# Adding the last experts' block results into two DRAM tables by indirect transfers, in place of storing them and gathering them

## The chip, the cores and the metric

The kernel runs on one core of one Trainium2 chip. The metric is the device time of one launch in microseconds (us). The kernel before takes 2686.56 us, the median of 3 runs (2667.9, 2686.56 and 2697.57).

## The reference, cut to what matters

Two layers run over 4096 tokens of width 256 (32 tiles of 128). Each layer is an attention followed by a mixture of experts. The change is in the last stage, the second mixture: 16 experts with hidden width 256, 4 chosen for each token, and in the attention before it, which routes the first 20 tiles.

```python
# z = x + attention; h = rms(z) * ff_ln_w
# scores = h @ wg;  top 4 of 16;  weights = softmax over the 4 chosen
# per token: y = sum over the 4 experts e of weight_e * (silu(h @ w1[e]) * (h @ w3[e])) @ w2[e]
# out = skip + tanh(g_ffn) * (z + y)
```

So every token gets four rows of expert output, each times its weight, added to its own row z.

## The kernel before, in words

The five stages run one after the other: softmax attention, first experts (8 experts, 2 chosen), linear attention, causal attention, last experts. Routing sorts tokens by expert: a token's normalised row is written by GpSimd (POOL) with an indirect transfer (`Router.send`, L360) to four places in the DRAM table `moe_rows`, one for each chosen expert, so that each expert's tokens stand in whole blocks of 128 rows. Places that no token takes keep the zeros that the softmax stage wrote there. The last experts have two parts: 20 tiles routed in the causal stage (95 blocks) and 12 tiles routed while the first part is computed (63 blocks); 158 blocks in all. The 12 tiles' rows need 48 sends.

One loop over blocks b is written out by hand on each engine of `experts`; there is no scheduler. TensorE (PE) in iteration i turns the rows of block i+2 (`turn_rows`, L1403, into `moe_pt`), does the gate and up products of i+1 (`up`, L1416, `moe_pgu`), turns the activation of i (`turn_act`, L1424) and does the down product of i-1 (`down`, L1435, `moe_py`). ScalarE (ACT) and VectorE (DVE) split the turned rows into a high and a low part (L1248, L1333), form silu times up (L1253, L1338), and DVE copies the block's result from PSUM into `moe_ys` (L1344, three buffers). SyncE (SP) loads block rows into `moe_xs` (`load_rows`, L1081, three buffers, behind a wait for `turn_rows` three blocks earlier).

ACT stores each block's result to a DRAM table (L1265). When all blocks of a part are stored, POOL gathers, for each tile and each k of 4, the 128 result rows by the tokens' slot numbers (`gather`, L1174, into `moe_yg`), and DVE combines (`combine`): four multiply-adds with the weights `wk` (L1315) and one with the gate and the skip row (L1323). SP loads z and skip (L1085, L1087) and stores the output (L1091). The first part's 20 tiles are combined between the blocks of the second part, one every second block, the second part's 12 tiles after the last block. For the first three of these 12 tiles (`HELD` is 3) POOL gathers rank by rank as soon as the experts concerned are stored (`limits`, `until`, L1202 to L1204). The weights `wk` by rank come from `share` and four times `share_of` (L338 to L343), in `weigh`.

## Time and profile before

| | |
|---|---|
| median of 3 runs | 2686.56 us |
| the profiled execution | 2682.36 us |
| its span | 2680.6 us |
| busy: PE, DVE, ACT, POOL | 2266.7, 1855.2, 1159.6, 1103.8 us |
| last experts, from its first instructions | from 2137 us to the end, 544 us |

The profiled execution's own time is 1.76 us over its span, and 4.2 us under the median. Times in the views are counted from the span's start. A row of a timeline gives the start, the duration, the engine, the line of the kernel, what is written and read, and in brackets how long the engine was idle before and what ended that. "DMA to landing" is counted from the start of the issuing instruction to the transfer's completion.

### The profile page before, as it was taken

The numbers are of one execution on the slowest core, as the hardware profiler recorded it, in microseconds if no ns is written. First come the engines' busy times: TensorE is split into PE (matmuls) and PEld (weight loads), VectorE is DVE, ScalarE is ACT, GpSimd is POOL, SyncE is SP. The second block draws the span as 40 slices with busy tenths as digits, with TensorE's granted clock in tenths as the row PEclk, the third lists the DMA queues.
The fourth block names the chain that finished last, engine by engine and source line by source line (L and its number), as shares of the span: only waits on it lengthen the run. The fifth ranks groups of instructions, "written<-read, shape, count | busy, mean of one in ns | idle before, by whom it ended". The sixth has DMA issues, their size and how long they took to land. (4 is left out here: it accounts for less than half of the span.)

```text
span 2680.6 us, 60407 instructions
## 1 busy us (share of the span) xinstructions
PE 2266.7 (85%) x20880; PEld 1718.4 (64%) x20880; DVE 1855.2 (69%) x3965; ACT 1159.6 (43%) x2509; POOL 1103.8 (41%) x1111
## 2 busy tenths in 40 slices
PE   6899999885887689995799998999988698999990
PEld 4555555543766567773577877777767577887770
DVE  4888888872556757765778788788787365445754
ACT  2676667664533223333344444444333263333330
POOL 3454445464153500000454454455477600224626
PEclk9897779865888889997999999999989799999995
DMA  5455555442368431201322323322334472446754
GB/s 118 120 115 129 143 129 135 114 125 87 113 215 252 150 134 41 60 29 40 88 66 75 84 66 78 81 72 73 76 96 116 136 240 79 138 137 184 234 159 144
DMA packets 249859, 313.10 MB, mean 117 GB/s; under 512 B 45152, under 2 KB 202848, under 8 KB 249056
## 3 DMA queue, kind: packets, MB, share of 16 engines
q1 hardware_dynamic: 188592, 219.11, 29.3%
q0 software_dynamic: 26624, 58.79, 8.0%
q10 hardware_dynamic: 34352, 31.34, 3.5%
q8 instruction: 180, 2.95, 0.5%
q14 instruction: 111, 0.91, 0.1%
HBM read 122.40 MB, written 102.24 MB: 84 GB/s over the span
## 5 line engine op out<-in xcount | busy, mean ns | idle before, releaser
L2084 POOL TENSOR_TENSOR ca_qk<-ca_qk,ca_q_swap 128x512 f32<-128x512 f32 x160 | 249.3, 1558 | 366.5 <-DVE ca_q_swap L2262 366.2
L731 DVE TENSOR_REDUCE soft_top<-soft_pa 128x2 fp32r<-128x512 f32 x512 | 328.1, 683 | 101.2 <-PE soft_pa L811 98.1
L626 ACT ACTIVATE soft_prob<-soft_pb 128x512 f32<-128x512 f32 x512 | 285.7, 594 | 190.4 <-PE soft_pb L804 187.9
L804 PE MATMUL soft_pb<-soft_rep 25*128 25x256 f32 x1024 | 210.2, 378 | 46.5 <-DVE soft_top L731 27.0
L804 PEld LDWEIGHTS soft_pb<-soft_rep 25*128 25x128 f32 x1024 | 137.3, 225 | 169.6 <-issue 85.3
L1416 PE MATMUL moe_pgu<-moe_w_hi,moe_xt_hi 128*128 x472 | 196.1, 415 | 38.9 <-DVE moe_xt_lo L1333 30.1
L811 PE MATMUL soft_pa<-soft_rep 24*128 24x256 f32 x1024 | 219.2, 384 | 5.8 <-DVE soft_top L731 3.5
L1435 PE MATMUL moe_py<-moe_w_d,moe_at 128*128 x788 | 217.8, 392 | 1.5 <-issue 0.8
L1338 DVE TENSOR_TENSOR moe_act_f<-moe_silu,moe_pgu 128x256 f32<-128x256 f32 (+1 forms) x236 | 88.4, 375 | 151.0 <-ACT moe_silu L1253 150.4
L2353 PE MATMUL ca_py<-ca_w_hi,ca_ot_hi 128*128 128x256 f32 x512 | 157.6, 308 | 35.0 <-DVE ca_ot_lo L2283 34.8
L1253 ACT ACTIVATE moe_silu<-moe_pgu 128x256 f32<-128x256 f32 (+1 forms) x236 | 82.1, 348 | 230.6 <-PE moe_pgu L1416 230.3
L825 PE MATMUL soft_po<-soft_prob,soft_vaug 128*32 128x256 f32 x2048 | 175.7, 473 | 0.0
L2262 DVE TENSOR_TENSOR ca_q_swap<-ca_q_swap,ca_sin_q 128x512 f32<-128x512 f32 x128 | 118.3, 924 | 80.8 <-DMA ca_q_swap<-ca_q_f 80.6
L1416 PE MATMUL moe_pgu<-moe_w_hi,moe_xt_lo 128*128 x472 | 174.1, 369 | 0.0
L1416 PE MATMUL moe_pgu<-moe_w_lo,moe_xt_hi 128*128 x472 | 173.7, 368 | 0.0
L2146 ACT ACTIVATE ca_ot_hi<-ca_po 128x512 fp32r<-128x512 f32 x128 | 69.5, 595 | 209.3 <-PE ca_po L2451 209.3
L1174 POOL DMA_INDIRECT moe_yg<-moe_ys_rows,moe_held x112 | 113.2, 1011 | 111.1 <-DVE moe_ys L1344 32.3
L360 POOL DMA_INDIRECT moe_rows<-moe_x_new,moe_held x80 | 78.1, 976 | 195.1 <-DVE moe_ys L1344 118.1
L2353 PE MATMUL ca_pp<-ca_ht_hi,ca_w_hi 128*128 128x512 f32 x312 | 138.7, 444 | 23.1 <-ACT ca_q_f L2132 19.6
L1333 DVE TENSOR_TENSOR moe_xt_lo<-moe_pt,moe_xt_hi 128x256 fp32r<-128x256 f32 x236 | 99.4, 421 | 74.8 <-ACT moe_xt_hi L1248 73.4
L2353 PE MATMUL ca_py<-ca_w_lo,ca_ot_hi 128*128 128x256 f32 x512 | 150.9, 295 | 0.0
L2353 PE MATMUL ca_py<-ca_w_hi,ca_ot_lo 128*128 128x256 f32 x512 | 150.6, 294 | 0.0
(377 smaller groups left out, 6376.3 us busy)
## 6 DMA issues: line engine op xcount, KB each, us to landing
ca_q_swap<-ca_q_f SPq DMA_DIRECT2D x640, 64.0 KB
moe_xs<-moe_rows SPq DMA_DIRECT2D x236, 128.0 KB, 2.1
soft_rep<-soft_parts SPq DMA_DIRECT2D x378, 64.0 KB
moe_rows<-soft_blank SPq DMA_DIRECT2D x27, 768.0 KB, 3.7
...
```

The lines of the kernel that those rows point to most:

```text
L626: act.activation(prob[:, k % 4, h, :], p_b[:, 2 * T * h:2 * T * (h + 1)], ACT.Exp).then_inc(prob_ready, 1)
L731: dve.tensor_reduce(heads[:, j, :, g], p_a[:, 2 * T * h:2 * T * (h + 1)].rearrange("p (c s) -> p c s", c=HALF), AX, ALU.max).then_inc(a_do ...
L804: mm = pe.matmul(p_b[:, out], rep[of, i % 4, g, at:at + PART], rep[of, i % 4, g, 0:T], start=True, stop=True)
L811: mm = pe.matmul(p_a[:, out], rep[of, n % 4, g, at:at + PART], rep[of, n % 4, g, T:2 * T], start=True, stop=True)
L825: mm = pe.matmul(p_o[g % 2][32 * j:32 * j + 32, 0:T], vaug[:, i % 4, sc, 4 * g + j, :], prob[:, (2 * g + j // 2) % 4, j % 2, sc * T:(sc + ...
L1174: pool.indirect_dma_start(out=yg[:, t % HELD, k, :], out_offset=None, in_=ys_rows[h], in_offset=bass.IndirectOffsetOnAxis(ap=slot_id[:, t, ...
L1333: dve.tensor_tensor(xt_lo[:, b % 2, :, :], p_t[b % 2][:, 0:DIM].rearrange("p (k t) -> p k t", k=KC), xt_hi[:, b % 2, :, :].bitcast(fp32), ...
L1416: mm = pe.matmul(p_gu[b % 2][:, 0:W2], x[:, b % 2, k, :], w, start=(n == 0), stop=(n == 3 * KC - 1))
L1435: mm = pe.matmul(p_y[b % 2][:, 0:DIM], at[:, b % 2, m, :], w_d[:, bass.ds(e, 1), m, :].rearrange("p a d -> p (a d)"), start=(m == 0), stop ...
L2084: pool.tensor_tensor(qk[:, u % 2, m, :], qk[:, u % 2, m, :], q_swap[:, p % 2, :], ALU.add).then_inc(qk_ready, 1)
L2262: dve.tensor_tensor(out.rearrange("p (b s) -> p b s", s=SEQ), src.rearrange("p (b s) -> p b s", s=SEQ), tab[int(m == RQ)][:].unsqueeze(1). ...
L2353: mm = pe.matmul(out, x, y, start=start and n == 0, stop=stop and n == len(todo) - 1)
```

## The change

- The weight goes with the row. A sent row of the last experts is now 273 words wide (`WIDE`): 256 values, its token's 16 weights by expert, and its token's number as an integer. `place` is followed at once by `share`, which writes weights and numbers into the rows; `share_of` and `limits` are gone for these experts.
- DVE evacuates a block with a multiplication by the weight column of the block's expert (L1405), taken with a register that it loads for each block (L1401), where it copied before.
- POOL adds the block's 128 result rows to a DRAM table by the token numbers in the block's rows (L1239, an indirect transfer with add). Even blocks add into table 0, odd ones into table 1. An add is issued behind a wait that the add two blocks earlier, into the same table, has landed (`out_of`). Table 0 holds z, written by the causal stage; table 1 is zeroed. Rows that no token took have weight zero and a number of 0 to 127, rows of padding ahead of the tokens.
- `moe_xs` has six buffers, since the number and the weights are read from it until the add is done; SP loads block b's rows behind a wait that block b-6 has been added, no longer behind `turn_rows`. DVE writes `moe_ys` of block n when block n-3 has been added.
- A tile's combination is one addition of the two tables' rows (L1367) and the operation with gate and skip (L1369); SP loads three tiles for it in place of two. ACT stores nothing, POOL gathers nothing.
- The softmax stage clears 23 pieces in place of 32. The causal stage fills the wide table with blank rows, three blocks at a time, in its first 53 steps, from SP. `until`, `reached` and the early gathers are gone.

In the fences below a row is one instruction in an engine's order of issue; `x` with a number means as many alike in a row. POOL, from the third `rstd` of the last experts' routing on, before and after:

```order
L167 TENSOR_TENSOR moe_r_rstd<-moe_r_var,moe_r_half_neg 128x4 x3
L360 DMA moe_rows<-moe_x_new,moe_held 8448x256 x48
L1174 DMA moe_yg<-moe_ys_rows,moe_held 128x256 x80
L1202 TENSOR_LOAD moe_until
L1202 ISA x2
L1204 TENSOR_TENSOR moe_spare<-moe_r_half_neg 1x1
L1174 DMA moe_yg<-moe_ys,moe_held 128x256 x3
```

```order
L368 DMA moe_rows<-moe_x_new,moe_held 8064x273
L1239 DMA moe_sums<-moe_ys,moe_xs 3072x256
L368 DMA moe_rows<-moe_x_new,moe_held 8064x273
L1239 DMA moe_sums<-moe_ys,moe_xs 3072x256 x17
L1239 DMA moe_sums<-moe_ys,moe_xs 2304x256 x63
```

The 48 sends stood in a row, paced by block results; they now alternate with the adds of blocks 30 to 78. 128 gathers became 158 adds.

DVE, the last blocks and what follows them (before, then after):

```order
L1333 TENSOR_TENSOR moe_xt_lo<-moe_pt,moe_xt_hi 128x256
L1338 TENSOR_TENSOR moe_act_f<-moe_silu,moe_pgu 128x256
L1344 COPY moe_ys<-moe_py 128x256
L1315 SCALAR_TENSOR_TENSOR moe_xd<-moe_yg,moe_held,moe_xd 128x256 x4
L1323 SCALAR_TENSOR_TENSOR moe_xd<-moe_xd,moe_gate,moe_sk 128x256
```

```order
L1389 TENSOR_TENSOR moe_xt_lo<-moe_pt,moe_xt_hi 128x256
L1394 TENSOR_TENSOR moe_act_f<-moe_silu,moe_pgu 128x256
L1401 TENSOR_LOAD moe_held
L1401 ISA x2
L1405 ISA
L1405 TENSOR_SCALAR moe_ys<-moe_py,moe_xs 128x256
```

A load of the expert's number into a register now stands between the activation and the evacuation of each block.

SP after its last load of rows (before, then after):

```order
L1091 DMA out<-moe_xd 128x256
L1085 DMA moe_xd<-scratch 128x256
L1087 DMA moe_sk<-scratch 128x256
L1091 DMA out<-moe_xd 128x256
```

```order
L1112 DMA moe_sk<-scratch 128x256 x5
L1120 DMA moe_xd<-moe_sums 128x256
L1120 DMA moe_xb<-moe_sums 128x256
L1132 DMA out<-moe_xd 128x256
L1112 DMA moe_sk<-scratch 128x256
L1120 DMA moe_xd<-moe_sums 128x256
L1120 DMA moe_xb<-moe_sums 128x256
L1132 DMA out<-moe_xd 128x256
```

The pair of table loads stands five times ahead of the first store; then store and three loads alternate seven times, and five stores end it.

The diff, cut to its core:

```diff
@@ -326,8 +325,14 @@
         dve.wait_ge(route, ticks.n)
         dve.reciprocal(wsum[:], wsum[:]).then_inc(route, ticks.one())
         dve.wait_ge(route, ticks.n)
-        dve.tensor_tensor(weight[:], weight[:], wsum[:].unsqueeze(2).to_broadcast([PART, n, E]), ALU.mult
-                          ).then_inc(route, ticks.one())
+        if self.carry:
+            dve.tensor_tensor(self.rows[:, :, DIM:DIM + E], weight[:], wsum[:].unsqueeze(2).to_broadcast([PART, n, E]), ALU.mult
+                              ).then_inc(self.wk_ready, 1)
+            dve.tensor_scalar(self.rows[:, :, DIM + E:].rearrange("p t o -> p (t o)").bitcast(U32), self.thr[:, 1:n + 1],
+                              self.order[:], None, ALU.add).then_inc(self.ids_ready, 1)
+        else:
+            dve.tensor_tensor(weight[:], weight[:], wsum[:].unsqueeze(2).to_broadcast([PART, n, E]), ALU.mult
+                              ).then_inc(route, ticks.one())
 
     def share_of(self, dve, k):
...
 
-        to = self.c["moe_rows"][self.h]
+        to = self.c[self.stage + "_rows"][self.h]
         if first == 0:
             pool.wait_ge(self.idx_ready, 1)
+            if self.carry:
+                pool.wait_ge(self.wk_ready, 1)
+                pool.wait_ge(self.ids_ready, 1)
         for n in range(first, min(last, self.n * self.TOP)):
             t, k = divmod(n, self.TOP)
...
@@ -1048,10 +1065,17 @@
             linear = LinearAttention(ahead, st)
         LATE = FIRST[1]
 
+        OUT = len(ys_out)
+
         def written(eng, blocks):
 
-            for i in range(3):
-                eng.wait_ge(ys_out[i], 16 * ((blocks - i + 2) // 3))
+            for i in range(OUT):
+                eng.wait_ge(ys_out[i], 16 * ((blocks - i + OUT - 1) // OUT))
+
+        def out_of(eng, b):
+
+            if b >= 0:
+                eng.wait_ge(ys_out[b % OUT], 16 * (b // OUT + 1))
 
         def combined_behind(b):
 
...
@@ -1077,14 +1101,31 @@
                     n = b - START[h]
                     if b == START[1]:
                         sp.wait_ge(route.sent, 16 * NEW * TOP)
-                    past(sp, xt_mm, b - 2)
-                    sp.dma_start(xs[:, b % 3, :], xs_rows[h][n * PART:(n + 1) * PART]).then_inc(xs_in[b % 3], 16)
+                    if adds:
+                        out_of(sp, b - XS)
+                    else:
+                        past(sp, xt_mm, b - 2)
+                    sp.dma_start(xs[:, b % XS, :], xs_rows[h][n * PART:(n + 1) * PART]).then_inc(xs_in[b % XS], 16)
+
+                def load_skip(t):
+                    past(sp, stored[t % SUMS], 16 * (t // SUMS))
+                    sp.dma_start(sk[:, t % SUMS, :], skip[t]).then_inc(xd_in[t % SUMS], 16)
+
+                def load_tables(t):
+                    h = int(t >= FIRST[1])
+                    if t == FIRST[h]:
+                        written(sp, START[h] + BLOCKS[h])
+                    at = PART * (t - FIRST[h] + 1)
+                    for dst, src in ((xd, tables[h][0]), (xb, tables[h][1])):
+                        sp.dma_start(dst[:, t % SUMS, :], src[at:at + PART, :]).then_inc(xd_in[t % SUMS], 16)
 
                 def load_sum(t):
+                    if adds:
+                        load_skip(t)
+                        load_tables(t)
+                        return
                     past(sp, stored[t % SUMS], 16 * (t // SUMS))
                     sp.dma_start(xd[:, t % SUMS, :], x_in[t]).then_inc(xd_in[t % SUMS], 16)
-                    if norm == "rms":
-                        sp.dma_start(sk[:, t % SUMS, :], skip[t]).then_inc(xd_in[t % SUMS], 16)
 
                 def store_sum(t):
                     sp.wait_ge(final, t + 1)
...
@@ -1144,8 +1187,14 @@
                 for t in behind:
                     if t not in [combined_behind(b - STORE_LAG) for b in range(ALL)]:
                         store_sum(t)
-                    if t not in [combined_behind(b - LOAD_LAG) for b in range(ALL)] and t + SUMS < TILES:
+                    if not adds and t not in [combined_behind(b - LOAD_LAG) for b in range(ALL)] and t + SUMS < TILES:
                         load_sum(t + SUMS)
+                if adds:
+                    for t in range(LATE, LATE + SUMS):
+                        load_skip(t)
+                    for t in range(LATE, LATE + SUMS):
+                        load_tables(t)
+
                 def last_sum(n):
                     t = LATE + n
...
                     ).then_inc(yg_in[t % HELD], 16)
 
+                if adds:
+                    for b in range(ALL):
+                        g = behind(b, MEASURE)
+                        if g is not None:
+                            route.root(pool, g)
+                        if b > PLACE:
+                            route.send(pool, b - PLACE - 1, b - PLACE)
+                        pool.wait_ge(y_ready, b + 1)
+                        out_of(pool, b - 2)
+                        h = part_of(b)
+                        pool.indirect_dma_start(
+                            out=tables[h][b % 2], out_offset=bass.IndirectOffsetOnAxis(
+                                ap=xs[:, b % XS, DIM + EXPERTS:].bitcast(U32), axis=0),
+                            in_=ys[:, b % 3, :], in_offset=None, bounds_check=tables[h][b % 2].shape[0] - 1, oob_is_err=True,
+                            compute_op=ALU.add).then_inc(ys_out[b % 2], 16)
+                    return
                 route.send(pool, 0, NEW * TOP, (y_ready, PLACE, START[1] - PLACE - 4))
                 pool.wait_ge(route.sent, 16 * NEW * TOP)
...
@@ -1298,8 +1349,11 @@
                             route.tally(dve)
                     if b == PLACE:
                         route.place(dve)
-                        route.limits(dve, until[:], START[1] + 3, until_ready)
-                    if b == WEIGH:
+                        if adds:
+                            route.share(dve)
+                    if b == WEIGH and adds:
+                        route.name_experts(dve)
+                    if b == WEIGH and not adds:
                         route.weigh(dve)
                         if norm == "layer":
                             dve.wait_ge(route.wk_ready, TOP)
...
                             dve.wait_ge(gated, 1)
 
                 def combine(t):
-                    dve.wait_ge(xd_in[t % SUMS], (32 if norm == "rms" else 16) * (t // SUMS + 1))
+                    dve.wait_ge(xd_in[t % SUMS], (48 if adds else 16) * (t // SUMS + 1))
+                    row = xd[:, t % SUMS, :]
+                    if adds:
+                        dve.tensor_tensor(row, row, xb[:, t % SUMS, :], ALU.add).then_inc(added, sums.one())
+                        dve.wait_ge(added, sums.n)
+                        dve.scalar_tensor_tensor(out=row, in0=row, scalar=gate[:], in1=sk[:, t % SUMS, :],
+                                                 op0=ALU.mult, op1=ALU.add).then_inc(final, 1)
+                        return
                     dve.wait_ge(yg_in[t % HELD], 16 * TOP * (t // HELD + 1))
-                    row = xd[:, t % SUMS, :]
                     for k in range(TOP):
                         past(dve, added, sums.n if k else 0)
                         op = dve.scalar_tensor_tensor(out=row, in0=yg[:, t % HELD, k, :], scalar=wk[:, t, k:k + 1], in1=row,
                                                       op0=ALU.mult, op1=ALU.add)
-                        if norm == "layer" and k == TOP - 1:
+                        if k == TOP - 1:
                             op.then_inc(final, 1)
                         else:
                             op.then_inc(added, sums.one())
-                    if norm == "rms":
-                        dve.wait_ge(added, sums.n)
-                        dve.scalar_tensor_tensor(out=row, in0=row, scalar=gate[:], in1=sk[:, t % SUMS, :],
-                                                 op0=ALU.mult, op1=ALU.add).then_inc(final, 1)
...
@@ -1339,9 +1395,17 @@
                                           p_gu[(b + 1) % 2][:, HIDDEN:W2], ALU.mult).then_inc(act_ready, 1)
                     if b >= 1:
                         n = b - 1
+                        if adds:
+                            if n == START[1]:
+                                dve.wait_ge(route.expert_ready, 1)
+                            e = dve.value_load(expert_of[0:1, n:n + 1], min_val=0, max_val=EXPERTS - 1)
                         dve.wait_ge(y_mm, n + 1)
-                        past(dve, ys_out[n % 3], 16 * (n // 3))
-                        dve.tensor_copy(ys[:, n % 3, :], p_y[n % 2][:, 0:DIM]).then_inc(y_ready, 1)
+                        out_of(dve, n - 3)
+                        if adds:
+                            dve.tensor_scalar(ys[:, n % 3, :], p_y[n % 2][:, 0:DIM], xs[:, n % XS, DIM:DIM + EXPERTS][:, bass.ds(e, 1)],
+                                              None, ALU.mult).then_inc(y_ready, 1)
+                        else:
+                            dve.tensor_copy(ys[:, n % 3, :], p_y[n % 2][:, 0:DIM]).then_inc(y_ready, 1)
                     routing(b)
                     t = combined_behind(b)
                     if t is not None:
...
@@ -2048,13 +2121,21 @@
                     if summed(n) is not None:
                         old, h = summed(n)
                         sp.wait_ge(zn_ready, 2 * old + h + 1)
-                        sp.dma_start(z_out[old * TPC + 2 * h:old * TPC + 2 * h + 2].rearrange("t p d -> p t d"),
+                        at = old * TPC + 2 * h
+                        part = int(at >= SENT)
+                        at = PART * (at - part * SENT + 1)
+                        sp.dma_start(c["moe1_sums"][part][0][at:at + 2 * PART, :].rearrange("(t p) d -> p t d", p=PART),
                                      z[:, old % ZB, 2 * h:2 * h + 2, :]).then_inc(stored[h], 16)
                     new = fresh(n, 0)
                     if new is not None and new >= 1:
                         load_x(new)
                     if n == 0:
                         held.load(sp)
+                        sp.wait_ge(blank_in, 16)
+                    if 0 <= n < len(empty):
+                        h, to = empty[n]
+                        sp.dma_start(to.rearrange("(r p) d -> p r d", p=PART),
+                                     blank[:].unsqueeze(1).to_broadcast([PART, to.shape[0] // PART, WIDE])).then_inc(emptied[h], 16)
                     if n == STEPS - 1:
                         sp.wait_ge(qk_ready, M5 * UNITS)
```

## Rows read from the trace of the kernel before

**Rows 1.** The page: the chain that ended last, share of the span by line.

```profile
PE moe_pgu L1416 7%; PE moe_py L1435 4%; DVE moe_xd L1315 2%; PE moe_pat L1424 1%; PE moe_pt L1403 1%; POOL moe_yg L1174 1%; DVE moe_xt_lo L1333 0%; DMA moe_xs<-moe_rows 0%; PE moe_py L211 0%; DMA moe_yg<-moe_ys,moe_held 0%; DVE moe_ys L1344 0%; PE moe_py L193 0%; PE moe_py L252 0%; DMA moe_ys<-moe_ys 0%; DVE moe_xd L1323 0%
```

**Rows 2.** Windows of L1344, one copy for each block: stretch, length, copies' busy time, clock, DMA share, GB/s.

```profile
2151.30:2187.53 36.23, 5.51 (x13) 1.00 0.94 314
2187.53:2283.02 95.49, 10.11 (x24) 0.95 0.28 90
2283.02:2452.28 169.26, 26.75 (x63) 1.00 0.44 142
2452.28:2575.71 123.43, 16.83 (x40) 1.00 0.76 226
2575.71:2613.32 37.61, 5.94 (x14) 1.00 0.41 126
```

**Rows 3.** Timeline of one block's period in the first part.

```profile
2298.94 0.38 PE L1403 MATMUL moe_pt<-moe_held,moe_xs 128*128 128x128 f32 x2
...
2300.77 1.03 PE L1435 MATMUL moe_py<-moe_w_d,moe_at 128*128 x4
...
2301.17 0.42 DVE L1338 TENSOR_TENSOR moe_act_f<-moe_silu,moe_pgu 128x256 f32<-128x256 f32 x1 [0.96 <-ACT moe_silu L1253]
2301.64 0.38 PE L1403 MATMUL moe_pt<-moe_held,moe_xs 128*128 128x128 f32 x2
...
2301.84 0.42 DVE L1344 COPY moe_ys<-moe_py 128x256 f32<-128x256 f32 x1 [0.25 <-PE moe_py L1435]
...
2303.03 0.97 POOL L360 DMA_INDIRECT moe_rows<-moe_x_new,moe_held  x1 [4.40 <-DVE moe_ys L1344]
```

**Rows 4.** Lines L1081 and L360 in 2300 to 2400: issues (duration in ns), then landing.

```profile
L1081 SPq DMA_DIRECT2D moe_xs<-moe_rows x37: 319/320/320, 2302.0 to 2398.8; - x37
DMA to landing us min/median/max: 2.0/2.1/3.6
...
L360 POOL DMA_INDIRECT moe_rows<-moe_x_new,moe_held x29: 971/972/974, 2303.0 to 2397.1; - x29
DMA to landing us min/median/max: 2.6/2.7/4.4
```

**Rows 5.** Line L1174, the gathers, in 2580 to 2610: issues, then landing.

```profile
L1174 POOL DMA_INDIRECT moe_yg<-moe_ys,moe_held x9: 998/1007/1010, 2587.9 to 2606.7; - x9
DMA to landing us min/median/max: 2.8/3.1/4.5
```

**Rows 6.** Line L1081 in 2150 to 2250, then in 2460 to 2570.

```profile
DMA to landing us min/median/max: 2.0/3.5/7.5
...
L1081 SPq DMA_DIRECT2D moe_xs<-moe_rows x36: 319/319/430, 2461.3 to 2569.8; - x36
DMA to landing us min/median/max: 2.1/2.9/4.0
```

**Rows 7.** Timeline of DVE: the first and the last operation of `share_of` in the last experts.

```profile
2267.81 0.36 DVE L338 TENSOR_TENSOR moe_r_left<-moe_r_key,moe_r_top 128x192 f32<-128x192 f32 x1
...
2272.32 0.35 DVE L343 TENSOR_REDUCE moe_held<-moe_r_left 128x12 f32<-128x192 f32 x1
```

**Rows 8.** Timeline of the end: last block's copy, one store and the loads behind it, the last gather.

```profile
2617.85 0.42 DVE L1344 COPY moe_ys<-moe_py 128x256 f32<-128x256 f32 x1 [0.44 <-PE moe_py L1435]
...
2661.37 0.34 SPq L1091 DMA_DIRECT2D out<-moe_xd  x1
...
2663.12 0.32 SPq L1085 DMA_DIRECT2D moe_xd<-scratch  x1
2663.49 0.43 SPq L1087 DMA_DIRECT2D moe_sk<-scratch  x1
...
2671.76 1.13 POOL L1174 DMA_INDIRECT moe_yg<-moe_ys,moe_held  x1 [0.30 <-issue]
2674.86 2.05 DVE L1315 SCALAR_TENSOR_TENSOR moe_xd<-moe_yg,moe_held,moe_xd 128x256 f32<-128x256 f32 x4 [2.84 <-DMA moe_yg<-moe_ys,moe_held]
2676.94 0.48 DVE L1323 SCALAR_TENSOR_TENSOR moe_xd<-moe_xd,moe_gate,moe_sk 128x256 f32<-128x256 f32 x1
```

**Rows 9.** Causal stage: line L338, and DVE's waits for the swapped halves; softmax stage: its clears.

```profile
L338 DVE TENSOR_TENSOR ca_r_left<-ca_r_key,ca_r_top x4: 476/482/486, 1968.1 to 2014.2; 128x320 f32<-128x320 f32 x4
...
DVE ca_q_swap L2262 <- DMA ca_q_swap<-ca_q_f: 80.6, 64, 3.6
...
moe_rows<-soft_blank SPq DMA_DIRECT2D x27, 768.0 KB, 3.7
```

162 lines of the change are left out of this document (82 added, 80 removed).

## The prediction

> **What bounds the kernel now.** I read the page's chain of waits first. In the last experts it runs through TensorE, with DVE's combinations and POOL's gathers behind [rows 1]. Then the windows over the copies of L1344, of which each block has one; they give the block's period by stretch [rows 2]: 36.23 / 13 = 2.79 us while the weights are prepared (A), 95.49 / 24 = 3.98 with the routing of the last 12 tiles (B), 169.26 / 63 = 2.69 in the rest of the first part (C), 123.43 / 40 = 3.09 where 20 combinations lie between the blocks (D), 37.61 / 14 = 2.69 after these (E). 2.69 is TensorE's own work: the turning of a block starts at 2298.94 and the next one's at 2301.64 [rows 3]. D's blocks are 0.40 longer, as a combination is five DVE operations. The other limit is the end [rows 8]: the last copy ends at 2618.27, the span at 2680.6, so 62.3 us follow in which TensorE is idle and POOL's gathers set the pace.
>
> **The end.** The change removes 39 late gathers and four of the five multiply-adds. In its place: the last add. It is issued 0.77 us after its copy (2302.26 to 2303.03 in [rows 3]) and takes 2.7 + e to land, where 2.7 is a plain indirect write of the same 128 rows [rows 4] and e what the add costs more. The last three copies come close together, so the last add also waits for the one two before: about 7.0 us in all at the e = 1.05 that I take below. Then SP issues ten table loads, 4.1 us at 0.32 to 0.43 each, before its first store. For seven tiles it then does a store, waits 1.75 us from the store's start until it has landed (2661.37 to 2663.12 [rows 8]) and issues three loads, 0.37 + 0.43 + 0.43: 2.98 a tile, 20.9 in all. A load lands in 2.1 [rows 4], the two DVE operations take 0.9, and from the last operation's end (2677.42) to the span's end there are 3.2 [rows 8]. Sum 7.0 + 4.1 + 20.9 + 2.1 + 0.9 + 3.2 = 38 against 62: **-24**. Here SP takes POOL's place as the bound.
>
> **The ring of six buffers.** This is the change's price, and nothing in the diff's wording says it. SP may load block b's rows only when block b-6 is added. Before, the load waited for the turning of b-3, and the copy, ACT's store and the gathers were beside the path. Now copy, add and load form a loop with TensorE's order. Its parts: from the start of a turning to the end of that block's copy, three periods, 3 x 2.69 = 8.07, and from the start of the fourth iteration to the copy's end 3.32 (2298.94 to 2302.26 [rows 3]); copy to issue on POOL 0.77; landing 2.7 + e; the load of the rows 2.1 [rows 4], after which the turning of b starts. With 0.2 for the register load (below) that is 17.16 + e. The loop spans six blocks, and six blocks of TensorE's work are 16.1. So even at e = 0 it is 1.0 too long, and the period becomes (17.16 + e) / 6. With the shortest landings seen in these rows (2.6, 2.0) and no register load it is 2.80.
>
> **What the add costs.** No row shows one. The least is e = 0, a plain indirect write, 2.7. The most is a gather followed by a write with one issue: a gather lands in 3.1 [rows 5], less its issue of 1.0, so e = 2.1. The add must read its destination before it writes, but the source is read in the same time, and rows of 1 KB are short against the fixed part. Neither end is nearer; I take the middle, 1.05, and the period is 18.2 / 6 = 3.04. A landing of 2.7 less 1.0 of issue leaves 1.7 in which data moves and is confirmed.
>
> The Trainium skill ("Collectives: The Full Stack", the bandwidth ceiling, on why ReduceScatter is half of AllGather) says that an add in a DMA costs not by its arithmetic but by its second source read, which goes through the same ring and halves the rate. No run here shows it. By it the 1.7 would at most double, e would be at most 1.7, and the sum 15 us higher than mine.
>
> By stretch: C, 63 x (3.04 - 2.69) = **+22**. E, 14 x 0.35 = **+5**. D: landings under load are longer, the rows' load 2.9 in place of 2.1 [rows 6]; the gathers that made most of the load are gone but each tile has a third load and the adds read twice, so I take half, 0.4, for the load and the same for the add: (18.2 + 0.8) / 6 = 3.17 against 3.09, x 40 = **+3**. The gain of the shorter combination (0.40 a block, 16 us) is thus lost to the loop. A: DMA is 94% busy [rows 2] and the rows' load takes 3.5 [rows 6]; with 1.4 more for it and 1.5 for the add the period is 21.1 / 6 = 3.5 against 2.79, x 13 = **+9**. B: long DVE steps let the loop catch up; only the eight intervals of some 2.7 pay 0.35: **+3**.
>
> **The smaller parts.** Weights by rank: the twelve operations of `share_of` take 2267.81 to 2272.67 [rows 7], all of it in TensorE's way, since DVE does its block work behind them; with `limits` gone and the numbers added that is **-5**. `share` only moves from one step to another. The sends on POOL: a send and an add are 0.97 + 0.30 each, 2.5 of a period of 3.04, so they fit, the add starting 0.8 behind its copy as before. The register load on DVE: between the start of the activation and the copy there are 0.67 us (2301.17 to 2301.84 [rows 3]) with DVE idle for 0.25; TensorE has the same load in each block and no gap in [rows 3]. Between nothing and the 1.0 of a POOL issue I take 0.2 of delay. In A, where DVE's four operations already fill the block, it would be seen whole, but the loop's 3.5 covers it. The Trainium skill ("DMA: Bandwidth & Descriptors", latency and other measured facts) gives a register load a floor of about 0.6 us; no row here has one; by it the delay would be 0.35 and the sum 3 us higher. ACT's stores go: nothing, since ACT waited in every block.
>
> The causal stage loses 4 x 3 DVE operations of 0.48, 5.8 us, and gets 53 writes of 419 KB on SP among the half-swaps that DVE waits 80.6 us for [rows 9]. -6 to +10, taken as 0. The softmax stage has 9 clears of 768 KB less of 32, 3.7 us each and hidden [rows 9]: 0, at the least -5. Rows of 1092 in place of 1024 bytes: 7% more on loads of 2.1, hidden in the rounding.
>
> **Sum.** 22 + 5 + 3 + 9 + 3 - 5 - 24 = +13. On the profiled execution's 2682.4 that is 2695. This execution is 4 us under the median of the runs, 2686.6, whose three runs lie 30 us apart, so I leave it at **2695**, no difference that can be told. About 1%, 27 us, is what a measurement of this kernel can tell: faster is under 2660, slower over 2713.
>
> **Rivals.**
> *The forecast*, the six-buffer loop at e from 0 to 2.1: each us of e is 138 periods / 6 = 23 us and 1.5 in the end, so 2670 to 2721, with its centre inside 1%. Chance 0.52.
> *The loop does not bind* (faster): the add lands like a plain write and the loads overlap better than my walk round the loop has it. TensorE keeps 2.69. Then D falls to 2.69 (-16), C, E and B cost nothing, A perhaps +3, end -26 (e = 0), weights -5: -44, 2638. For it: TensorE is 100% in C, and the loop misses by only 1.0 in 16. Against it: the shortest landings in [rows 4] still give 2.80 (and with that 2660). Chance 0.22.
> *The two tables' chain binds* (slower): an add waits until the add two blocks back has landed, so the period is at least (0.77 + 2.7 + e) / 2 = 1.74 + e / 2. It overtakes the loop where 1.74 + e / 2 = 2.86 + e / 6, at e = 3.4, a landing of 6.1; the period is then 3.43: C +47, E +10, D +14, A +9, B +6, weights -5, end -20: +61, 2743, and more beyond. For it: gathers land in up to 4.5 even here [rows 5], and the read before the write comes in no row. Against it: e would be over both bounds. Chance 0.18.
> *The causal stage decides*: the blank writes delay half-swaps by a good part of their worth, or its DVE saving counts: 10 to 20 us to either side of 2695. Chance 0.08.
>
> Faster takes the second rival and a little of the forecast's lower end and of the fourth: 0.24. Slower takes the chain, the forecast's part over e = 1.8 and some of the fourth: 0.31. The rest, 0.45, is within 1%. The range is 2650 to 2740: it holds the forecast's own 2670 to 2721 and leaves out half of the fast case and half of the slow one.
>
> **What would show it.** The evacuations of L1405 in C: 3.04 apart if I am right, 2.69 for the second case, 3.4 for the third. Who releases the turning: the load of the rows in the forecast; in the third case POOL's adds would be issued on the landing of an add, not on the copy. The landing of L1239: 3.7 by my middle. D's period: 3.17. The end: 38 us from the last evacuation, stores 2.98 apart. Wrong would be: a period that stays at 2.69 with adds that land in 3.5 or more, for then my loop has a part that is not there; or a difference in the stages before 2137 us.

## The result, and the profile after

The changed kernel takes **2850.68 us** (median of 4 runs, 2824.22 to 2855.78), the kernel before, on the same chip, 2685.8 (4 runs): 1.060 times as long, 95% interval 1.0512 to 1.0688. I had forecast 2695 with a range of 2650 to 2740, so the forecast is wrong, on the slow side and by 156 us. The profiled execution of the changed kernel took 2855.78 us, its span is 2854.0, against 2680.6 before.

Where the 173.4 us between the two spans lie: the last experts start 5.0 us later (ScalarE's gate at 2142.24, before at 2137.23); from that start to the end of the last evacuation they take 668.9 us, before 481.0 (+187.9); and what follows the last evacuation takes 42.8 us instead of 62.3 (-19.5). So nearly all of it is the pace of the blocks, and the end did gain, though less than forecast.

The page's chain of waits by line, which answers to [rows 1]. First the shares by engine, then by line.

```profile
DMA 11%; PE 7%; issue 3%; DVE 2%; SPq 1%; ACT 0%; DVEq 0%; POOL 0%; POOLq 0%; ACTq 0%
DMA moe_sums<-moe_ys,moe_xs 7%; PE moe_pgu L1477 4%; DMA moe_xs<-moe_rows 4%; PE moe_py L1496 2%; DVE moe_ys L1405 1%; PE moe_pt L1464 1%; DMA out<-moe_xd 1%; PE moe_pat L1485 0%; SPq L1120 0%; ACT moe_silu L1304 0%; DVE moe_act_f L1394 0%;
```

Before, TensorE's lines led. Now the first item is the landing of the adds, and the third that of the row loads: two transfers which stood beside the path before.

Windows over L1405, the evacuation of each block, cut at the same block numbers as [rows 2]: stretch, length, evacuations' busy time with their count, granted clock, DMA share, GB/s.

```profile
2156.27:2217.01 60.74, 6.29 (x13) 0.89 0.76 197
2217.01:2319.45 102.44, 11.61 (x24) 0.97 0.42 76
2319.45:2576.26 256.81, 30.50 (x63) 0.94 0.50 99
2576.26:2743.34 167.08, 19.36 (x40) 0.93 0.55 113
2743.34:2805.22 61.88, 6.78 (x14) 0.89 0.43 77
```

| stretch | blocks | period before | forecast | after | forecast's us | measured us |
|---|---|---|---|---|---|---|
| A | 13 | 2.79 | 3.5 | 4.67 | +9 | +24.5 |
| B | 24 | 3.98 | 4.1 | 4.27 | +3 | +7.0 |
| C | 63 | 2.69 | 3.04 | 4.08 | +22 | +87.6 |
| D | 40 | 3.09 | 3.17 | 4.18 | +3 | +43.7 |
| E | 14 | 2.69 | 3.04 | 4.42 | +5 | +24.3 |

Periods are length over count (C: 256.81 / 63 = 4.08), the last column is the difference of the two lengths. The five sum to 187 of the 188 us. In C the kernel has little but blocks and sends, and DMA is 0.50 busy at a granted clock of 0.94: nothing there is full, and still a block takes 1.4 us more than TensorE needed before. That is how a ring that is too short looks here.

The chain of waits through three blocks of stretch D, piece by piece: start, duration, what.

```profile
2591.46 3.79 DMA moe_sums<-moe_ys,moe_xs
2595.27 2.62 DMA moe_xs<-moe_rows
2597.89 0.04 issue
2597.94 0.44 PE moe_pt L1464 x2
2598.38 0.42 issue
2598.79 2.37 PE moe_pgu L1477 x6
2601.16 0.43 PE moe_pat L1485 x2
2601.59 1.58 PE moe_py L1496 x4
...
2603.30 0.50 DVE moe_ys L1405
...
2604.56 4.43 DMA moe_sums<-moe_ys,moe_xs
2609.01 3.56 DMA moe_xs<-moe_rows
```

Read it as a circle. An add lands (3.79 us), a buffer is free, SyncE loads the rows of a later block into it (2.62), TensorE turns these rows, and in the same pass of its loop, right behind, it does the down projection of the block three before, whose evacuation (0.50) lets the next add go. From add to add it is 2604.56 - 2591.46 = 13.1 us, and three blocks of the program go by in it, not six.

One such pass on TensorE, in the timeline: start, duration, engine, line, what, and in brackets the idle time ahead and what ended it. Then windows of all engines: length, PE, PEld, DVE, ACT, POOL busy (count), clock, DMA share, GB/s.

```profile
2597.94 0.44 PE L1464 MATMUL moe_pt<-moe_held,moe_xs 128*128 128x128 f32 x2 [2.47 <-DMA moe_xs<-moe_rows]
2598.79 0.49 PE L1477 MATMUL moe_pgu<-moe_w_hi,moe_xt_hi 128*128 x1 [0.42 <-issue]
...
2600.11 0.63 PE L1477 MATMUL moe_pgu<-moe_w_lo,moe_xt_hi 128*128 x1
...
2601.38 1.77 PE L1496 MATMUL moe_py<-moe_w_d,moe_at 128*128 x4
2602.99 0.38 PE L1464 MATMUL moe_pt<-moe_held,moe_xs 128*128 128x128 f32 x2
...
2603.68 0.39 PE L1477 MATMUL moe_pgu<-moe_w_hi,moe_xt_lo 128*128 x1
```

```profile
2597.90:2601.60 3.70, 3.25 (x11) 2.43 (x12) 0.42 (x1) 0.77 (x2) 0.55 (x1) 0.71 0.84 209
```

TensorE has been idle for 2.47 us. Its first products still go at the old pace, but the later ones of the up projection take 0.63 us in place of 0.39, and the down projection takes 1.77 in place of 1.03 [rows 3]. The granted clock is 0.71 in this stretch, a mixture of the two levels of 2.4 and 1.2 GHz, where it is 1.00 in [rows 2] for the stretch C of before. So in this pass the stall lengthens the loop that causes it: from the turning's start to the evacuation's end it is 5.86 us here (2597.94 to 2603.80), and 3.32 in [rows 3].

The add and the load of the rows by line, in 2490 to 2560 (the add: issues with their duration in ns, landing) and in 2300 to 2400 (the add's landing; the load). They answer to [rows 4].

```profile
L1239 POOL DMA_INDIRECT moe_sums<-moe_ys,moe_xs x17: 1542/1542/1561, 2490.5 to 2555.0; - x17
DMA to landing us min/median/max: 3.5/3.9/4.5
...
DMA to landing us min/median/max: 3.7/3.8/4.7
...
L1108 SPq DMA_DIRECT2D moe_xs<-moe_rows x25: 319/320/320, 2302.5 to 2397.5; - x25
DMA to landing us min/median/max: 2.0/2.1/3.4
```

An add lands in 3.8, of which I had said 3.7, and the load in 2.1, of which I had said 2.1. The add's landing, the one unknown that carried my range, was right.

What waits, in the whole stage (2130 to 2860), and SyncE's queue (2500 to 2770): engine, line waited for, us in total, times, longest.

```profile
POOL moe_sums L1239 <- DVE moe_ys L1405: 287.5, 107, 14.9
PE moe_pt L1464 <- DMA moe_xs<-moe_rows: 119.6, 62, 18.8
POOL moe_sums L1239 <- DMA moe_sums<-moe_ys,moe_xs: 51.3, 19, 3.8
...
SPq L1108 <- DMA moe_sums<-moe_ys,moe_xs: 207.5, 60, 10.6
```

GpSimd waits for evacuations, not for the add two before (287.5 against 51.3 us), so the chain of the two tables is not the main bound. SyncE waits 207.5 of these 270 us for adds, with the row loads behind it.

The end, on SyncE: first the last evacuation, the first table load, the first store, then one tile's turn and the last stores. It answers to [rows 8].

```profile
2810.69 0.48 DVE L1405 TENSOR_SCALAR moe_ys<-moe_py,moe_xs 128x256 f32<-128x256 f32 x1 [1.27 <-DMA moe_sums<-moe_ys,moe_xs]
...
2817.61 0.32 SPq L1120 DMA_DIRECT2D moe_xd<-moe_sums  x1
...
2822.24 0.43 SPq L1132 DMA_DIRECT2D out<-moe_xd  x1
...
2830.00 0.43 SPq L1132 DMA_DIRECT2D out<-moe_xd  x1
2832.22 0.32 SPq L1112 DMA_DIRECT2D moe_sk<-scratch  x1
...
2848.28 2.92 SPq L1132 DMA_DIRECT2D out<-moe_xd  x5
```

### The profile page after: what moved, and what is told of

The parts are those of the page before. It is cut to its first block and busy times, and to the rows that moved or that the text cites. A ratio compares the mean times of both kernels' runs of the same rounds, so it can differ in the third digit from the quotient of the medians.

```text
span 2854.0 us, 60996 instructions
## 1 busy us (share of the span) xinstructions
PE 2330.3 (82%) x20880; PEld 1731.8 (61%) x20880; DVE 1810.2 (63%) x3842; ACT 1162.1 (41%) x2509; POOL 1224.9 (43%) x1137
## 5 line engine op out<-in xcount | busy, mean ns | idle before, releaser
L1239 POOL DMA_INDIRECT moe_sums<-moe_ys,moe_xs x158 | 248.2, 1571 | 357.0 <-DVE moe_ys L1405 287.5
L1477 PE MATMUL moe_pgu<-moe_w_hi,moe_xt_hi 128*128 x472 | 205.3, 435 | 61.6 <-issue 39.6
L1496 PE MATMUL moe_py<-moe_w_d,moe_at 128*128 x788 | 227.7, 407 | 1.1 <-issue 1.0
L1464 PE MATMUL moe_pt<-moe_held,moe_xs 128*128 128x128 f32 x472 | 102.6, 302 | 146.5 <-DMA moe_xs<-moe_rows 146.0
L1299 ACT ACTIVATE moe_xt_hi<-moe_pt 128x256 fp32r<-128x256 f32 x236 | 90.4, 383 | 252.6 <-PE moe_pt L1464 247.6
L1464 PEld LDWEIGHTS moe_pt<-moe_held,moe_xs 128*128 128x128 f32 x472 | 63.8, 153 | 195.4 <-DMA moe_xs<-moe_rows 179.3
L1477 PE MATMUL moe_pgu<-moe_w_hi,moe_xt_lo 128*128 x472 | 182.1, 386 | 0.0
L836 PE MATMUL soft_po<-soft_prob,soft_vaug 128*32 128x256 f32 x2048 | 182.0, 487 | 0.0
L1477 PE MATMUL moe_pgu<-moe_w_lo,moe_xt_hi 128*128 x472 | 182.0, 386 | 0.0
L1477 PEld LDWEIGHTS moe_pgu<-moe_w_hi,moe_xt_hi 128*128 128x128 f32 x472 | 97.0, 205 | 106.8 <-issue 97.9
```

The lines of the kernel that those rows point to most:

```text
L836: mm = pe.matmul(p_o[g % 2][32 * j:32 * j + 32, 0:T], vaug[:, i % 4, sc, 4 * g + j, :], prob[:, (2 * g + j // 2) % 4, j % 2, sc * T:(sc + ...
L1239: pool.indirect_dma_start(out=tables[h][b % 2], out_offset=bass.IndirectOffsetOnAxis(ap=xs[:, b % XS, DIM + EXPERTS:].bitcast(U32), axis=0 ...
L1464: mm = pe.transpose(p_t[b % 2][:, k * PART:(k + 1) * PART], xs[:, b % XS, k * PART:(k + 1) * PART], ident)
L1477: mm = pe.matmul(p_gu[b % 2][:, 0:W2], x[:, b % 2, k, :], w, start=(n == 0), stop=(n == 3 * KC - 1))
L1496: mm = pe.matmul(p_y[b % 2][:, 0:DIM], at[:, b % 2, m, :], w_d[:, bass.ds(e, 1), m, :].rearrange("p a d -> p (a d)"), start=(m == 0), stop ...
```

## The experiments

My theory from the trace, "Theory 1" in the expectations: the loop advances three blocks, since TensorE works three blocks ahead in order, so the period is the loop's length over (buffers - 3). In every kernel below the evacuations have one line for all blocks, and I read the same 63 blocks (stretch C).

**1. Five and seven buffers.** Label xs5 and xs7.

```diff
-    XS = 6 if adds else 3
+    XS = 5 if adds else 3      # xs5
+    XS = 7 if adds else 3      # xs7; the router's tile `kept` lies in the gap, to make room
```

> The changed kernel with five row buffers. Theory 1 (loop over buffers minus 3 = 2 blocks): the period becomes 11.8 / 2 = 5.9 and 12.9 / 2 = 6.4 us, some 2 us more for 120 blocks and about as much in the early ones: 270 to 320 us more, about 3150. Theory 2 (the prediction's six-block loop): (17.2 + 1.2) / 5 = 3.7, no more than now. Rival 3 (POOL or the tables' chain): no change, 2851.

> The changed kernel with seven row buffers in place of six; nothing else but the place of one small tile differs. Theory 1 (loop over three blocks: in one iteration TensorE turns block n+3's rows and does block n's down product, block n is then evacuated, added, and frees the buffer of block n+6, so the loop advances buffers minus 3 blocks): the period of the changed kernel, 3.93 us late in the first part and 4.31 in the second, times 3 is a loop of 11.8 and 12.9; over 4 blocks that is 2.95 and 3.2, where the first part is then held at 3.17 by a send and an add on POOL (1.03 + 0.30 + 1.54 + 0.30). 68 x 0.75 + 51 x 1.1 + some 10 to 20 in the first 40 blocks: 115 to 130 us less, about 2725. Theory 2 (the prediction's loop, six blocks with three of them at TensorE's own 2.69): it can't explain 3.9 at six buffers; it would give (17.2 + 1.2) / 7 = 2.63, so TensorE's 2.69 everywhere. Rival 3 (POOL's issue, or the wait for the add two blocks back, sets the period): no change, 2851.

Measured: xs5 3217.36 us (1 run), 67 over the 3150 expected. xs7 2716.96 (4 runs, 2709.62 to 2721.18; 2725 expected), 1.0131 of the kernel before, interval 1.0087 to 1.0175. The window of stretch C in xs5, then in xs7:

```profile
2394.52:2806.39 411.87, 30.49 (x63) 0.76 0.32 62
```

```profile
2287.10:2492.64 205.54, 30.49 (x63) 0.98 0.62 125
```

Periods of 6.54, 4.08 and 3.26 for 5, 6 and 7 buffers. Times 2, 3 and 4 this is 13.1, 12.2 and 13.0 us. The last of these is not a clean measure, though: in the blocks of C that have a send, GpSimd in xs7 issues adds and sends back to back, 3.17 us a pair with the 0.30 between two issues, so that it and not the loop sets the pace there. Stretch D has no sends. Its periods are 6.63, 4.18 and 3.25, and times 2, 3 and 4 they are 13.3, 12.5 and 13.0: one loop of some 13 us, shared among buffers less three. Times 5, 6 and 7, as my prediction had it, the periods of C are 32.7, 24.5 and 22.8, which is no constant, and it would have put xs5 at 18.2 / 5 = 3.6.

The evacuations show the number of blocks in a turn directly. In xs5 they come in pairs: they start at 2468.40 and 2471.10, at 2481.22 and 2483.97, at 2494.49 and 2497.24, so two blocks every 13 us. In the changed kernel they often come in threes, 2.7, 2.7 to 3 and then 5 to 7 us apart. One buffer, 1092 bytes of each partition, is worth 134 us.

**2. A plain indirect write in place of the add.** Label plain.

```diff
-                            in_=ys[:, b % 3, :], in_offset=None, bounds_check=..., oob_is_err=True,
-                            compute_op=ALU.add).then_inc(ys_out[b % 2], 16)
+                            in_=ys[:, b % 3, :], in_offset=None, bounds_check=..., oob_is_err=True
+                            ).then_inc(ys_out[b % 2], 16)
```

> The changed kernel with the indirect transfer writing the rows in place of adding them (so the sums over a token's experts are left out); same rows, same waits. It measures what the add itself costs. Theory 1: landing falls from 3.9 to 2.7 us and the issue from 1.54 to 0.97; the three-block loop is 1.2 shorter, 0.4 us a block, over 150 blocks 60 us: about 2790, with the periods still at 3.5 and 3.9. Rival 3 (POOL's issue is the bound): 0.57 a block, 90 us less. Rival 4 (the read before the write, and its load on the DMA engines, is what costs the 165 us): the time falls to the kernel before's 2686 or below.

Measured: 2761.66 (1 run), 89 us under the changed kernel and still 75 over the kernel before. Its line for this transfer in 2300 to 2400:

```profile
L1239 POOL DMA_INDIRECT moe_sums<-moe_ys,moe_xs x30: 972/972/975, 2301.3 to 2398.8; - x30
DMA to landing us min/median/max: 2.4/2.4/3.5
```

The same rows to the same places land in 2.4 without the add and in 3.8 with it: e is **1.4**, of which 0.57 is the longer issue on GpSimd (1.542 against 0.972). A third of 1.4 is 0.47 a block; the period in C goes from 4.08 to 222.10 / 63 = 3.53, so 0.55. The rest may be the clock, which rises from 0.94 to 0.98; no run separates it. The gain of 89 us was more than the 60 expected. The lesson is in the 75 us that remain: had the add cost no more than a plain write, the change would still be slower, through the loop.

**3. Take the add out of the loop.** Label keep. The buffer was held for 17 small columns: the weights and the token number. ScalarE and VectorE now copy these to rings of twelve, and the row buffer is free when it is turned and copied. Four row buffers are then enough.

```diff
-    XS = 6 if adds else 3
+    XS = 4 if adds else 3
+    KEEP = 12
@@ load_rows, SyncE
-                        out_of(sp, b - XS)
+                        for kept in (xt_mm, kw_ready, kn_ready):
+                            past(sp, kept, b - XS + 1)
@@ the add, GpSimd
-                                ap=xs[:, b % XS, DIM + EXPERTS:].bitcast(U32), axis=0),
+                                ap=kn[:, b % KEEP:b % KEEP + 1], axis=0),
@@ behind the turning of block b + 2, ScalarE
+                        act.activation(kw[:, (b + 2) % KEEP, :], xs[:, (b + 2) % XS, DIM:DIM + EXPERTS], ACT.Copy).then_inc(kw_ready, 1)
@@ the same, VectorE
+                        at_ = (b + 2) % KEEP
+                        dve.tensor_copy(kn[:, at_:at_ + 1], xs[:, (b + 2) % XS, DIM + EXPERTS:].bitcast(U32)).then_inc(kn_ready, 1)
```

> The changed kernel with the tie between the row buffers and the adds cut: ScalarE copies a block's 16 weights and VectorE its token numbers to small tiles (12 blocks deep) when the rows are turned, so the row buffers, four now, are free after that. All adds and waits between them stay. Theory 1: the three-block loop is gone. TensorE's 2.69 returns where POOL doesn't send; where a send goes with each add (48 blocks) POOL's 3.17 binds. Against the kernel before: +0.48 x 48 = +23, the combinations between blocks -16, weights by rank -5, end -20, start of the stage +5, evacuations waiting for the register load 0 to +10: 2675 to 2690. Rival 3 (POOL or tables' chain): 2800 or more. Rival 4 (the adds' load on the DMA engines): 2800 or more.

Measured: **2674.44** (10 runs, 2662.27 to 2684.91), 0.9963 of the kernel before (0.9933 to 0.9994). Against the changed kernel, 176 us are back with the add, its landing, the wider rows, the register load and both tables all in place. The window of stretch C:

```profile
2288.82:2483.17 194.35, 30.48 (x63) 0.98 0.67 132
```

The period is 3.08. The time is at the fast end of the 2675 to 2690 expected, and far from both rivals' 2800. That the wait for an add lay in the loads' path is thereby shown, and that neither the adds' load on the DMA engines nor the two tables' chain made the 165 us, since both are still there.

**4. The register load.** Label nold.

```diff
-                            e = dve.value_load(expert_of[0:1, n:n + 1], min_val=0, max_val=EXPERTS - 1)
...
-    xs[:, n % XS, DIM:DIM + EXPERTS][:, bass.ds(e, 1)],
+    xs[:, n % XS, DIM:DIM + 1],
```

> The changed kernel, six row buffers, but the evacuation takes a constant column of the weight row, so VectorE loads no register (the outputs carry the wrong weight). Theory 1 (the loop over three blocks: turning, up, down, evacuation, add, landing, load of the buffer, then turning again): the 0.3 to 0.6 us that the register load puts in front of the evacuation leaves the loop and each block gets a third of that, 0.10 to 0.20 us, over some 120 blocks that are bound by it: 2826 to 2838 us, from 2850. Theory 2 (each load's full time stands in every block, in series with TensorE): 158 x 0.3 to 0.6, so 2755 to 2803.

Measured: 2840.2 (2 runs, 2831.13 to 2849.28), 10 us under the changed kernel, whose own runs lie 32 us apart, and above the 2826 to 2838 of Theory 1. In the profiled executions it is 637.0 against 654.4 from the first evacuation to the last, 17.4 us or 0.11 a block. But stretch C, with 63 blocks, shows nothing of it (257.5 against 256.8), and sendlate below, which keeps the load, is 5 us under the changed kernel there and 10 us in stretch E alone. So Theory 2 is out, and a gain of 0.11 a block isn't told from the differences between executions. The load itself, in the changed kernel:

```profile
L1401 DVEq TENSOR_LOAD <-moe_held x17: 300/304/316, 2494.2 to 2558.7; - x17
L1401 DVEq FUSED_REGOPS  x17: 190/190/190, 2494.5 to 2559.0; - x17
```

0.49 us in sum, in front of each evacuation. In the pass shown above it was hidden: the load starts at 2601.6 and its last step at 2602.2, and the down projection that the evacuation waits for ends at 2603.17. (The Trainium skill, "DMA: Bandwidth & Descriptors", latency and other measured facts, gives a floor of about 0.6 us for such a load. In this trace the load alone takes 0.30, and only with the register steps behind it does it come near that.)

**5. The send behind the add.** Label sendlate.

```diff
-                        if b > PLACE:
-                            route.send(pool, b - PLACE - 1, b - PLACE)
                         pool.wait_ge(y_ready, b + 1)
                         ...
                         pool.indirect_dma_start(... compute_op=ALU.add).then_inc(ys_out[b % 2], 16)
+                        if b > PLACE:
+                            route.send(pool, b - PLACE - 1, b - PLACE)
```

> The changed kernel, six row buffers, with the send of the second half's rows (48 blocks, one a block) issued by GpSimd behind the block's add and not in front of it. Theory 1 (loop over three blocks): the send held the add back by up to 1.4 us in those 48 blocks, a third of that a block is won where the evacuation finds GpSimd idle: 48 x 0.3 to 0.45 = 14 to 22 us, about 2832. The period in the 48 blocks is then about 3.6 and not 3.97. Theory 2 (GpSimd's own time, 3.17 us for a send and an add, and not its order, sets the pace there): no change, 2850.

Measured: 2850.28 (2 runs), no change. Theory 1's figure for this edit was a miss: the period over the blocks with sends was 4.08 in sendlate and 3.97 in the changed kernel, not 3.6. The changed kernel's 17 blocks without a send behind these 47 have 3.95, so no cost of the sends is seen there; in sendlate the same 17 have 3.71, so a cost of 0.37 a block isn't excluded. Nor is Theory 2's reason right, since the period is well over 3.17. Why an add held back by up to 1.4 us costs nothing in the time isn't shown; the evacuations come in bunches (2.7, 2.7, then 6), and GpSimd is idle between the bunches.

**6. What bounds keep now.** Four edits, each from a wait in its trace. The tail first, label keep_tail: SyncE issues the loads for tile t + 4 behind the store of tile t, so it need not see that store land.

```diff
                         store_sum(t)
-                        if t + SUMS < TILES:
-                            load_sum(t + SUMS)
+                        lag = 1 if adds else 0
+                        if n >= lag and t - lag + SUMS < TILES:
+                            load_sum(t - lag + SUMS)
```

> The kernel with the weights and token numbers kept in a ring of twelve and four row buffers (2674 us), with one edit: in the tail, SyncE issues the loads of tile t+4 behind the store of tile t, so that it no longer waits for the landing of the store it has just issued (2.0 to 2.5 us a tile, stores 3.4 to 3.5 us apart). Theory: the bound becomes DMA, 5.6 MB at the 250 GB/s seen at peak in this tail, 23 us, so the 36 us from the last add's landing to the end fall to 26 to 28: 2664 to 2667. Rival: the tail is bound by the loads' latency whatever the order, 2674.

Measured: 2668.8 (10 runs), 0.9946 of the kernel before (0.992 to 0.9971), a little over the 2664 to 2667 expected. By the time alone it can't be told from keep, whose interval overlaps this one. The profile tells it: from the last evacuation's end to the span's end it is 34.8 us, and 42.8 in keep; from the first table load behind the last add's landing it is 28.4 and 36.0, where 26 to 28 was expected. DMA moved 204 GB/s over the last 27.6 us, not 250, so DMA at its peak is not shown to be the bound.

Then the tables' loads alone (label keep_spread) and a fourth result buffer alone (label keep_ys4):

```diff
-    STORE_LAG, LOAD_LAG = 4, 5
+    STORE_LAG, LOAD_LAG = 4, 6 if name == "moe1" else 5
...
-                    if b == START[1] + (4 if adds else 0):
-                        for t in range(SUMS):
-                            load_sum(t)
+                    t = b - START[1] - 4
+                    if adds and 0 <= t < SUMS:
+                        load_sum(t)
```

```diff
-        xs, ys = sb("xs", [PART, XS, WIDE if adds else DIM], of=own), sb("ys", [PART, 3, DIM], of=own)
+        xs, ys = sb("xs", [PART, XS, WIDE if adds else DIM], of=own), sb("ys", [PART, 4 if adds else 3, DIM], of=own)
...
-                        out_of(dve, n - 3)
+                        out_of(dve, n - (4 if adds else 3))
```

> The kernel with kept weights and token numbers and four row buffers (2674 us), with the loads of the tables alone changed: the first five tiles' loads at one tile a block, and later ones two blocks behind their store. Theory (SyncE's queue makes the row loads late): the stall of 9.3 us at block 100 falls to that of other blocks, and the period of blocks 120 to 143 from 2.9 to 2.7, -6 to -11 us. Rival (the adds' landings and the three result buffers make the stall there, VectorE waited 14.7 us for adds): -6 at the most, with blocks 120 to 143 unchanged.

> The same kernel (2674 us), with a fourth result buffer alone. Theory (SyncE's queue): blocks 96 to 143 as they were, -0 to -3 in all. Rival (result buffers): VectorE's 101 us of waits for the adds' landings shrink, and blocks 120 to 143 fall to 2.7.

Each ran once (2688.88 and 2664.77 us), and the stages before the last experts differ by up to 21 us between these executions, so I read the periods. keep_tail is the same as keep until the tail, so its difference from keep shows what two executions differ by; best and best2, below, have both edits, and their sends are spread further (they end before block 96).

| blocks | keep | keep_tail | keep_spread | keep_ys4 | best | best2 |
|---|---|---|---|---|---|---|
| 96 to 120 | 2.98 | 2.99 | 2.72 | 2.97 | 2.71 | 2.77 |
| 120 to 144 | 2.87 | 2.74 | 2.87 | 2.71 | 2.71 | 2.84 |
| first to last evacuation, us | 485.8 | 483.2 | 479.6 | 475.8 | 475.6 | 473.0 |

For the first row the theory of SyncE's queue holds. The fifteen loads in a row made the stall at block 100, here in keep:

```profile
2466.58 0.32 SPq L1124 DMA_DIRECT2D moe_xd<-moe_sums  x1
...
2473.34 11.99 SPq L1112 DMA_DIRECT2D moe_xs<-moe_rows  x6
```

From 2466.58 to 2473.3 SyncE issues nothing for the blocks. The interval at block 100 is 9.3 us in keep, 7.8 in keep_tail and 9.1 in keep_ys4, and 2.7 to 3.0 in the three kernels that spread the loads.

For blocks 120 to 144 the loads are not the cause, since keep_spread has keep's 2.87. That it is the number of result buffers is not shown either. Without a fourth buffer they take 2.87, 2.74 and 2.87, with it 2.71, 2.71 and 2.84. In best2 VectorE waits 27.4 us for the landings of adds between 2463 and 2587 although it has four buffers, and 0.9 us in best between 2473 and 2592, with the same instructions in these blocks. What makes them 0.13 longer in some executions stays open.

**7. All four together.** Label best, with the 48 sends at four in five blocks, and best2, at nine in ten.

```diff
-                            route.send(pool, b - PLACE - 1, b - PLACE)
+                            at_ = b - PLACE - 1
+                            route.send(pool, at_ * 4 // 5, (at_ + 1) * 4 // 5)      # best
+                            route.send(pool, at_ * 9 // 10, (at_ + 1) * 9 // 10)    # best2
```

> The kernel with kept weights, token numbers and four row buffers, with four edits: the tail's loads one store later (-8 to -10 us); the first five tiles' loads one tile a block and not fifteen loads in a row, and later loads two blocks and not one behind their store (-6 to -10: the stall of 9.3 us at block 100, and SyncE's waits for store landings in blocks 120 to 143, 14.7 us); the 48 sends at four in five blocks (-5 to -10: GpSimd's 3.1 us for send and add is no longer the pace of 48 blocks); a fourth result buffer (-5: VectorE waits for add landings in the first 16 blocks and in blocks 120 to 143). Sum 24 to 35: 2640 to 2650, under the kernel before (2686) by 1.3 to 1.7%. Rival: the chain of adds into the two tables, (1.56 + 3.9)/2 = 2.7 us a block, is already the pace, so that buffers and order give nothing before the tail: 2662.

> All four edits as before, with the 48 sends at nine in ten blocks instead of four in five. At four in five they ended at block 90, and the first load of the second half, which waits for the last of them, made a stall of 15.7 us at block 92. At nine in ten they end at block 84. Theory: the stall goes, 11 to 13 us, and GpSimd's work up to block 84 (48 x 1.33 + 53 x 1.84 = 161 us, against 53 x 2.69 = 143) still leaves blocks 60 to 84 at 3.1: 2652 to 2656, 0.988 to 0.990 of the kernel before. Rival: GpSimd is so far behind that the last send lands late again, 2660 to 2665.

Measured: best 2664.99 (7 runs, 2654.17 to 2669.15), 0.9916 (0.9884 to 0.9949), which was short of the 2640 to 2650 expected. It is near the 2662 of the rival, but not for the rival's reason: its blocks ran at 2.71 from 96 on with TensorE busy 108.62 of the 108.62 us of stretch D at a clock of 1.00, so TensorE and not the chain of adds sets that pace. (The rival's 2.7 counted the issue twice, since a landing of 3.9 is counted from the start of the issue.) What kept it from 2640 to 2650 is in part a new stall, an interval of 15.7 us at block 92: the sends now ended at block 90, and the first load of the second half waits for the last of them. GpSimd in best, near its end:

```profile
2394.52 1.54 POOL L1249 DMA_INDIRECT moe_sums<-moe_ys,moe_kn  x1 [0.30 <-issue]
2396.36 1.03 POOL L368 DMA_INDIRECT moe_rows<-moe_x_new,moe_held  x1 [0.30 <-DVE moe_ys L1423]
```

An add and a send take 1.54 + 0.30 + 1.03 + 0.30 = 3.17 us, over TensorE's 2.69; my prediction had 2.5 for the two. Once the add is out of the loop, GpSimd is the bound of these blocks: in keep it issues the two in turn from 2300 to 2330 with only these 0.30 between, and the 17 blocks behind the sends go at 2.67.

With nine in ten, **best2 takes 2657.23** (6 runs, 2647.91 to 2662.53), 0.9891 of the kernel before (0.9858 to 0.9923), 1.1% faster than the kernel before and 193 us under the changed one. It is just over the 2652 to 2656 expected. The stall is gone, but the intervals of best and best2 overlap, and stretch D took 114.01 us in best2 and 108.62 in best. Its windows, cut as above:

```profile
2146.38:2186.99 40.61, 6.27 (x13) 0.96 0.95 269
2186.99:2280.97 93.98, 11.59 (x24) 0.93 0.50 94
2280.97:2463.42 182.45, 30.47 (x63) 1.00 0.68 133
2463.42:2577.43 114.01, 19.32 (x40) 1.00 0.84 183
2577.43:2613.84 36.41, 6.77 (x14) 1.00 0.63 109
```

C is at 2.90, where the kernel before has 2.69; D at 2.85, where it has 3.09; E at 2.60 (a late evacuation stands right before it). So the idea of the change does gain in D and at the end, and pays in C with GpSimd's issues and in A, 40.61 us against 36.23, which I did not take apart.

## Why the prediction was wrong

**The ring of six buffers** is the step that failed. I had written the loop as three periods plus 17.16 - 8.07 = 9.09 us of other parts, plus e, and then put in TensorE's own 2.69 for these three periods. But they are periods of the very loop that was being worked out: while TensorE waits in order, the three blocks that it is ahead stretch with it. With P for the period, 6 P = 3 P + 9.09 + e, so P = (9.09 + e) / 3. With my own e = 1.05 this is 3.38, not 3.04, and with the landing of 3.8 that was measured, 0.05 more, it is 3.40. That one line makes C +45 instead of +22. It also takes away the comfort that I drew from the formula: a us of e costs 138 / 3 = 46 us and not 23. With nothing else put right, my sum would be about +72 in place of +13 (C +43, E +10, D +22, A +20, B +6, weights and end as they were), so 2754. That is outside my range, and still 97 us short.

The rest, from 3.40 to 4.08, is a mis-sized term in the same sum: turning to evacuation at 3.32. That is TensorE at full clock with a wait nowhere. In the loop of 13.1 us above the parts are 3.79 for the add, 2.62 + 0.04 for the load, 5.86 from the turning to the evacuation's end, 0.76 to the next add. Against my 3.75, 2.1, 3.32 and 0.77 the big one is 5.86. Of the 2.54 us that it is longer, 1.66 are the products from the first of the up projection to the end of the down projection at the lower clock (4.38 against 2.72; a pass of nold at a clock of 1.00, also behind a wait for rows, takes 2.76 for them). 0.71 lie between the start of the turning and the first of these products, and the trace names no wait for them. 0.17 are the evacuation. The 0.2 that I had added for the register load is not in this pass, as its load is over before the down projection ends. I had looked at the time of a pass that never stalls, and used it for one that always does.

The other steps:
- **What the add costs**: right. Landing 3.8 against 3.7, e = 1.4 against 1.05, inside 0 to 2.1; over the 2.7 that I had for a plain write it is 1.1, as that write lands in 2.4 here. The Trainium skill's rule ("Collectives: The Full Stack", the bandwidth ceiling, on ReduceScatter: the second source read halves the rate) gave an estimate of at most 1.7, and the 1.4 is within it. But 0.57 of it is GpSimd's issue, of which the rule says nothing; the part behind the issue grew by 0.83, and no run shows that it is the second read.
- **The stretches**: all five signs were right and all sizes too small, since each was a difference to a period with / 6 and with 3.32 in it. In D the median landings under load are hardly longer (3.9 for the add, 2.2 for the rows, where I had added 0.4 to each), but the row loads that stand on the chain take 2.6 and 3.56: they are issued among table loads.
- **The end**: right in kind, 42.8 against 38. Last evacuation to first table load 6.4 (7.0 forecast), loads to first store 4.6 (4.1), seven tiles 26.0 (20.9), the rest 5.7 (6.2). The term that was short is a tile's turn, 3.7 and not 2.98: a store takes 2.1 to 3.0 to land and not 1.75.
- **The sends fit**: wrong as a sum, 3.17 and not 2.5, since an add's issue is 1.54 and I had used the 0.97 of a write, and a send's is 1.03. No cost of it is seen in the time of the changed kernel, whose period was longer (sendlate), and it became the bound in xs7 and keep.
- **The register load**: 0.49 on VectorE's queue, for which I took a delay of 0.2. nold shows at most 17 us of it, and none in stretch C, so the delay is not measured. I had also written that no row has such a load; the trace of the kernel before has four of them on GpSimd (L1202), 0.30 for the load and 0.15 for the step behind it, which would have been the better guide.
- **Stages before**: the start of the last experts moved by 5.0 us, within the 10 allowed. In the executions of the experiments, with the same stages ahead, it lies anywhere from 2129.9 to 2151.5 (2137.2 before), so no difference can be told.
- **Rivals**: the tables' chain, my slow case, gave 2743 and did not come in: 51.3 us of GpSimd's waits against 287.5. What came was my own mechanism, with three blocks in a turn and a longer turn, and no case of mine held it: I let e alone carry the uncertainty, and took the structure of the formula as certain.

My statement of what would prove me wrong was too weak as well. It named a period that stays at 2.69; a period above 3.4 with a landing of 3.8, which is what came, is as plain a sign that a part of the loop was counted wrongly.
